# Four graph networks on one core: loops written out, selectors in PSUM, and one count matrix read by transposing DMAs

## What is computed

```python
x = _layernorm(x + _L0_gnn_ref(x, relation_emb, edge_index, edge_type))   # hyperbolic messages, 2 hops
x = _layernorm(x + _L1_gnn_ref(x, edge_index, edge_weight, ...))          # GRU, 2 rounds
x = _layernorm(x + _L2_gnn_ref(x, edge_index, ...))                       # SAGE convolution, 2 layers
x = _layernorm(x + _L3_gnn_ref(x, edge_index, ...))                       # SAGE convolution, 2 layers
```

```python
# L1, round t, with row = src and col = dst
agg = segment_sum(concat([x[col], x[row], edge_attr]) @ msg_W[t].T + msg_b[t], row)
x = gru_cell(agg, x, ...)
# L2, L3, each layer
agg = segment_sum(h[src], dst) * inv_deg
```

## Time and profile before

| | us |
|---|---|
| median of three runs | 22,558.81 |
| the profiled execution | 22,546.55 |
| its span, first to last instruction | 22,544.4 |
| sort, 116 to 3,241 | 3,125 |
| building the matrix, 3,357 to 6,996 | 3,639 |
| hyperbolic passes, each | 3,680 and 3,710 |
| dense pass 2 | 966 |
| dense pass 3, with the transposed copy | 1,999 |

### The profile page before, as it was taken

One profiled execution on the slowest core, in us unless ns is written; L12 is line 12 of the kernel. 1 busy time (PEld: TensorE's weight loads), 2 busy tenths in 40 slices (PEclk: granted clock), 3 DMA queues, 4 the chain that ended last, 5 costly groups with the idle time before them and its releaser, 6 DMA issues. The chain is left out here.

```text
span 22544.4 us, 302048 instructions
## 1 busy us (share of the span) xinstructions
PE 12710.9 (56%) x103818; PEld 11283.5 (50%) x103819; DVE 8510.4 (38%) x15488; ACT 2879.7 (13%) x5263; POOL 8346.1 (37%) x6810
## 2 busy tenths in 40 slices
PE   2222225333322555555555555488777788878887
PEld 1111114333322444444444444388677687878787
DVE  4444446444442555555455555501434400010101
ACT  0000000000001222222122222100343300000000
POOL 4444447888886555554455555300000000000000
PEclk6555556555555555555555555599999999999998
DMA  9600014333332222222222222297899697989798
GB/s 358 272 1 1 1 32 111 77 77 77 77 71 45 71 69 72 71 71 62 69 70 70 70 71 71 54 339 271 297 334 340 236 336 273 316 294 347 263 322 305
DMA packets 2131032, 3586.46 MB, mean 159 GB/s; under 512 B 554444, under 2 KB 1429728, under 8 KB 2037429
## 3 DMA queue, kind: packets, MB, share of 16 engines
q1 hardware_dynamic: 1732405, 3389.59, 42.5%
q0 software_dynamic: 397504, 181.65, 6.6%
HBM read 2672.91 MB, written 907.26 MB: 159 GB/s over the span
## 5 line engine op out<-in xcount | busy, mean ns | idle before, releaser
L762 POOL DMA_INDIRECT room<-table_hyp,pay x3328 | 3430.5, 1031 | 1116.5 <-issue 984.3
L1026 PE MATMUL pair<-room,side 128*128 x6656 | 1688.3, 435 | 2973.9 <-ACT side L1354 2432.6
L1121 PE MATMUL pair<-room,side 128*128 128x192 bf16 x30694 | 3049.1, 250 | 508.0 <-DMA side<-back 327.1
L749 POOL DMA_INDIRECT adj<-sc x1664 | 2962.8, 1781 | 791.9 <-issue 485.3
L1026 PEld LDWEIGHTS pair<-room,side 128*128 128x128 f32 x6656 | 1480.7, 327 | 3287.6 <-issue 3287.6
L1121 PE MATMUL pair<-room,onehot 128*128 128x192 bf16 x31058 | 3006.1, 247 | 110.4 <-DMA onehot<-back 74.8
L1121 PEld LDWEIGHTS pair<-room,side 128*128 128x128 f16 x30694 | 2664.5, 100 | 593.3 <-issue 453.8
L1121 PEld LDWEIGHTS pair<-room,onehot 128*128 128x128 f16 x31058 | 2629.1, 98 | 193.7 <-issue 138.1
L791 POOL DMA_INDIRECT sc<-table_lin,heavy_idx x6 | 5.7, 950 | 6957.4 <-DMA table_lin<-room 6957.4
L734 POOL DMA_INDIRECT payload<-room x1600 | 1554.9, 972 | 1685.7 <-DVEq L1706 1094.9
L2254 DVE TENSOR_REDUCE acc<-pair 128x384 f32 (+2 forms) x314 | 145.3, 526 | 4300.0 <-PE pair L1121 4296.7
(11 more groups left out here) (437 smaller groups left out, 18105.7 us busy)
## 6 DMA issues: line engine op xcount, KB each, us to landing
onehot<-back SPq DMA_DIRECT2D x308, 1024.0 KB, 7.7
side<-back SPq DMA_DIRECT2D x280, 1024.0 KB, 7.7
onehot<-back SPq DMA_DIRECT2D x264, 896.0 KB, 7.1
side<-back SPq DMA_DIRECT2D x240, 896.0 KB, 7.3
onehot<-head_hots SPq DMA_DIRECT2D x208, 1024.0 KB
adj<-xs SPq DMA_DIRECT2D x99, 1728.0 KB
adj<-xs SPq DMA_DIRECT2D x99, 1600.0 KB
side<-adj SPq DMA_DIRECT2D x148, 1024.0 KB, 8.6
```

The costliest lines, as they stand in the source:

```text
L749: pool.indirect_dma_start(out=adj_flat[q // 2][:, :], out_offset=bass.IndirectOffsetOnAxis(ap=edge_to[i % 2][q][:, t:t + 1], axis=0), in_= ...
L762: pool.indirect_dma_start(out=rows[:, h, t, :], out_offset=None, in_=table_hyp[:, :], in_offset=bass.IndirectOffsetOnAxis(ap=pay[:, h, t, ...
L1026: last = nc.tensor.matmul(ps_head[:, j * TW:j * TW + TW], sel_t[:, q % 2, j * P:j * P + P], flat_tab[:, bass.ds(b * TW, TW)], start=True, ...
L1121: last = nc.tensor.matmul(banks[c // 2][:, D3 * (c % 2):D3 * (c % 2) + D3], block_, x3[:, sources[k], :], start=j + k == 0 and c % 2 == 0, ...
```

## The change

Three things at once.

First, all loops over registers become Python loops, and every wait is on a constant; the tick semaphores go. The same work is issued in the same order. Second, `heavy_on` (two selectors of 128x128) moves from SBUF to PSUM, and DVE copies each group's keys to PSUM before it compares with them. Third, there is one matrix `mat`, with the source nodes as rows. The convolutions read it as they read `back`; the GRU passes load it through `dma_start_transpose`; the transposed copy of pass 3 and all that served it go. The heavy row for the GRU passes is a small array of its own, loaded by a plain DMA behind the last unit of each sweep.

```diff
-        def await_reg(eng, who, s, v):
-            eng.wait_ge(s, v)
-            eng.sem_inc(tick[who], 1)
+        def until(eng, s, v):
+            if v > 0:
+                eng.wait_ge(s, v)
...
-                with pool.Fori(0, ITERS - 1) as i:
+                for i in range(0, ITERS - 1):
...
-        heavy_on = [flat_x[:, 1024 + P * k:1024 + P * k + P] for k in range(2)]
+        heavy_on = [bank[2][:, P * k:P * k + P] for k in range(2)]
+        ps_own_keys = [bank[2][:, 2 * P + G * h:2 * P + G * h + G] for h in range(2)]
...
                 dve.drain().then_inc(key_made, 1)
+                V.tensor_copy(ps_own_keys[h], ekey[h])
                 V.tensor_tensor(srcf[h], srcf[h], pad_, ALU.add)
-                V.tensor_scalar(b_, lo_, P - 1, None, ALU.bitwise_and)
-                stt(a_, dstf[h], float(COLS[n % STREAMS // 2]), tile_colf[:, tiles_], ALU.mult, ALU.add)
+                V.tensor_scalar(a_, lo_, P - 1, None, ALU.bitwise_and)
+                V.tensor_scalar(far_block, far_, 7, None, ALU.arith_shift_right)
+                V.tensor_scalar(b_, far_, P - 1, None, ALU.bitwise_and)
+                dve.drain()
+                stt(edge_row, tile_colf[:, tiles_], float(P), a_, ALU.mult, ALU.add)
+                stt(a_, edge_row, float(NB), far_block, ALU.mult, ALU.add)
...
-                V.tensor_tensor(same[h], keys_on[h].rearrange("p (t e) -> p t e", e=P), over(ekey[h], P), ALU.is_equal)
+                V.tensor_tensor(same[h], keys_on[h].rearrange("p (t e) -> p t e", e=P), over(ps_own_keys[h], P), ALU.is_equal)
...
-            for b in range(ADJ_ROWS):
-                for v in range(2):
-                    sp.dma_start(adj[v][P * b:P * b + P, :], zeros_dram[:, 0:COLS[v] * P]).then_inc(zeroed, 16)
+            for v in range(2):
+                for b in range(COLS[v]):
+                    for u in range(2):
+                        half_ = slice(NB * P // 2 * u, NB * P // 2 * u + NB * P // 2)
+                        sp.dma_start(mat[v][P * b:P * b + P, half_], zeros_dram[:, 0:NB * P // 2]).then_inc(zeroed, 16)
+                sp.dma_start(heavy_near[v], zeros_dram[:, 0:COLS[v] * P]).then_inc(zeroed, 16)
...
-                    sp.dma_start(ring[r][:, 0:kn, 0:w * P], mats[half_ if v is None else v][:, k0:k0 + kn, at]).then_inc(unit_here[r], 16)
+                    if v is None:
+                        sp.dma_start_transpose(ring[r][:, 0:far, 0:w * P], mat[half_][near, P * k0:P * k0 + P * far]).then_inc(unit_here[r], 16)
                     else:
...
+                        sp.dma_start(ring[r][:, 0:kn, 0:w * P], mat[v].rearrange("(k p) c -> p k c", p=P)[:, k0:k0 + kn, near]).then_inc(unit_here[r], 16)
+                    if far < kn:
+                        sp.dma_start(ring[r][:, far, 0:w * P], heavy_near[half_][:, near]).then_inc(unit_here[r], 16)
...
-                            flips = turning and k0 + k < NB
-                            if flips:
-                                for t in (turn_act, turn_dve):
-                                    await_(t, NB * s + k0 + k + 1, i, 2 * NB)
...
-                                    flip = nc.tensor.matmul(o[:, P * (c % 4):P * (c % 4) + P], block_, ident16, start=True, stop=True)
```

More of the change, by code:

```diff
@@ L98, with __init__ @@
 class Shape:
-    def __init__(self, units, stages):
+    def __init__(self, units, sweeps):
         self.units = units
-        self.stages = stages
+        self.sweeps = sweeps
         self.n = len(units)
[L106 to L114, removed]
 def far_sources(half_, k):
@@ L728, in _ @@
             pool.wait_ge(filled, GROUPS * 16)
-            with pool.Fori(0, GITERS) as i:
+            for i in range(0, GITERS):
                 for h in range(2):
-                    await_reg(pool, "pool", staged, 2 * i + (h + 1))
+                    until(pool, staged, 2 * i + (h + 1))
                     for c in range(HC):
@@ L975, in _ @@
                     degrees(k, 0, h, h + k == 0)
-            with pe.Fori(1, NITERS + 1) as i:
+            for i in range(1, NITERS + 1):
                 for h in range(2):
@@ L981, in _ @@
                 q_step(i - 1)
-            with pe.Fori(NITERS + 1, GITERS) as i:
+            for i in range(NITERS + 1, GITERS):
                 for h in range(2):
@@ L1072, in run_pass @@
                 fetch_group(m, 0, 0)
-                with pe.Fori(0, ITERS - 1) as i:
+                for i in range(0, ITERS - 1):
                     fetch_group(m, i, 1)
@@ L1179, in gru @@
                 gates(0, 0, False)
-                with pe.Fori(0, NITERS // 2 - 1) as i:
+                for i in range(0, NITERS // 2 - 1):
                     for h in range(2):
@@ L1223, in conv @@
                 second_layer(0, 0, False)
-                with pe.Fori(0, NITERS // 2 - 2) as i:
+                for i in range(0, NITERS // 2 - 2):
                     for h in range(2):
@@ L1395, in run_pass @@
                     pass
-                with act.Fori(0, ITERS - 1) as i:
+                for i in range(0, ITERS - 1):
                     group(2 * i, 0, steps(2 * i + 1, 1))
@@ L1468, in gru @@
                 turned(1, 1)
-                with act.Fori(0, NITERS // 2 - 1) as i:
+                for i in range(0, NITERS // 2 - 1):
                     for h in range(2):
@@ L1501, in conv @@
                 hidden(1, 1, False)
-                with act.Fori(0, NITERS // 2 - 2) as i:
+                for i in range(0, NITERS // 2 - 2):
                     for h in range(2):
@@ L1795, in make_q @@
             def make_q():
-                with dve.Fori(0, NITERS) as i:
+                for i in range(0, NITERS):
                     keep_q(i, 1)
@@ L1801, in _ @@
             rsum(relblk[:, :, D], rel_sq)
-            with dve.Fori(1, NITERS + 1) as i:
+            for i in range(1, NITERS + 1):
                 for h in range(2):
@@ L1811, in _ @@
             dve.drain().then_inc(table_ready, 1)
-            with dve.Fori(NITERS + 1, GITERS) as i:
+            for i in range(NITERS + 1, GITERS):
                 for h in range(2):
@@ L2405, in gru @@
                 stage_blocks(1, 1, False)
-                with dve.Fori(0, NITERS // 2 - 1) as i:
+                for i in range(0, NITERS // 2 - 1):
                     for h in range(2):
```

361 lines of the change are left out of this document (123 added, 238 removed).

## The result

The changed kernel takes 21,236.87 us (median of 4 runs, 21,235.51 to 21,247.06), the kernel before 22,562.22 us beside it: ratio 0.9414, interval 0.9397 to 0.943. It is faster by 1,325 us, a third of the 3,957 us that the sum promised; the time lies in the range, near rival A (21,740).

The account below looks back on a forecast made before the run. No engine was full overall: DMA bound the dense passes, POOL the matrix building, a stall the sort and hyperbolic passes. 22,546.6 - 1,050 - 2,100 - 400 - 407 = 18,590 us; own range 17,700 to 19,500, with rivals 17,700 to 22,000.

Parts of the forecast that it names:

- rival A: Sort and hyperbolic passes: the stall stays, belonging to POOL's back-to-back issue; 21,740 us; chance 0.22, with B 0.05.
- Part 1 and 2: Straight programs without register waits end the stall: -1,050 us in the sort, -2,100 us in the hyperbolic passes.
- the stall: Sort and hyperbolic passes: PE's semaphore updates don't come through while POOL issues DMAs; 27.07 us in one hyperbolic group.
- Part 3: Matrix building: compare operands in PSUM bring the mean accumulating DMA from 1.781 to 1.542 us, -400 us.
- Part 4 and 5: Dense passes 2 and 3: no transposed copy, -1,033 us; transposing loads at 1,279 us a pass; together -407 us.
- my middle: Rate taken for transposing loads in dense passes 2 and 3, between two profile rows: 268 GB/s, 1,279 us a pass.
- the row of 256-byte pieces: Profile row of the output's store, 215 GB/s, taken as slow bound for transposing loads: 1,592 us a pass.
- Part 6: The rest: zeroing, edge additions, loop ends in dense passes, small GRU and convolution loops; 0, at best -50 us.
- B: Dense passes 2 and 3: transposing loads don't overlap, 2,621 us a pass, total 21,270 us; chance 0.13.
- C: Dense passes 2 and 3: each 256-byte row costs 59.9 ns, 5,004 us a pass, total 26,040 us; chance 0.07.

Follow-up runs that it names:

- The fastest version: The changed kernel with POOL waiting for landings after every eighth gather of the hyperbolic passes and every eighth scatter of the sort: 19,563.76 us (0.8674).

## Why the prediction was wrong

*Part 1 and 2, -1,050 and -2,100: the failed step.* I read the stall as "what several register waits at once do to the other engines while POOL issues DMAs". Written out with constants, the kernel before gains 82 us in the sort and 615 in the hyperbolic passes, and the stall stays. The sentence of rival A was the right one: it belongs to POOL's unbroken issue. That the building stage escapes because its DMAs are spaced by 1.85 us fits this, but no run changed that spacing. Against A I set the 40 fast matmuls 54 us after the slow ones, with POOL issuing in both. I had not looked at what POOL did in between. It began a stream of 40 scatters at 1466.69 and the next at 1553.21, after standing still for 36 us:

```profile
1466.69 0.97 POOL L734 DMA_INDIRECT payload<-room  x1 [23.25 <-DVEq L1706]
1553.21 0.97 POOL L734 DMA_INDIRECT payload<-room  x1 [35.77 <-DVEq L1706]
```

PE was slow 38 us into the first stream and fast 5 us into the second. The rows that I held against A speak for it. The sizes can only be compared with the pauses in place. The fastest version has its two passes at 5,538 us where the kernel before has 7,281, and the sort at 2,557 instead of 3,125. That is 2,311 us of the 3,150 that parts 1 and 2 promised; a group takes 53 us and not 47, and POOL's waits for its landings are 7 of these 53.

*Part 3, -400: mechanism right, size off.* The mean of the accumulating DMA is 1,544 ns, the forecast's 1.54 us, and POOL is busy 394 us less. But the stage lost 245 us: 275, as the run with this part alone undone shows, less the 30 by which DVE's new address instructions and the new layout make the stage longer; I had put these at nothing. I counted DVE's waiting as the room for part 3 and left out POOL's own wait, in each of four streams, for its last DMA to land: 91 us in the earlier trace rows, 244 after. A faster issue reaches that landing sooner.

*Part 4 and 5, -407: one term mis-sized.* A plain pass is 937 us as soon as the program is written out. A transposing pass takes 1,427 us, not 1,279: 240 GB/s, within the bounds (966 and 1,592), about half way between my middle and the row of 256-byte pieces. Two passes make 296 us, all of the miss. Against the written-out kernel, no copy and transposing loads are worth 935 + 1,932 - 1,427 - 1,426 = 14 us: what the copy cost, the transposes take back. The Trainium skill, "DMA: Bandwidth & Descriptors", section "Latency and other measured facts", gives 261 GB/s for a non-contiguous middle dimension; that was nearer than my middle (268). For the contiguous case it gives some 350 to 400 GB/s. The measurement doesn't agree: the ring's tile has the gap only in sweeps of 6 and 7 columns, and with it the loads ran at 239 GB/s, without it at 242.

*Part 6, 0 to -50: wrong.* I took the DMA engines as full (share 1.01), so that loop ends could cost nothing. Written out, a plain pass moves 366 GB/s instead of 354; the six passes lose some 230 us and the short steps some 90.

*The sum by its measured terms:* 22,547 - 1,019 (written out) - 303 (PSUM) + 30 (new addresses and layout) - 14 (no copy, transposes) = 21,241 us, against 21,237 measured. The rivals: A was right in its mechanism. Its 21,740 left out the 1,019 us of the written-out program and had parts 3 to 5 520 us too good (807 for 287), hence some 500 us too high. That the time came near it is in part luck: two errors offset each other. B fell: 364 transposing loads take 1,427 us, not 2,621. C fell: by the working of its 59.9 ns, a 256-byte packet took 1.14 x 16 x 1,427 us / 1,326,000 = 20 ns of an engine, not 60.

## What to carry to other kernels

When one engine issues DMAs back to back for tens of microseconds and the others show idle time with nothing awaited or with a "remote" releaser, put a pause into the issue before rewriting anything else: here three waits a group, two lines of code, gave 1,650 us where rewriting 25 loops gave 1,019. Find the length by trial; 8 DMAs (10 us) was best here, 6 and 11 were both 560 us and more behind. And a gain in the issue of a chain of DMAs counts only until the wait for landing ends last. Before a row is held against a rival, look at what the suspected engine did in between.

## What the runs showed of the hardware that was not expected

- PE's semaphore updates reached DVE and ACT 11 and 21 us late while POOL issued indirect DMAs every 1.24 us; with a pause of about 2 us every 5 us they passed within 0.6 us.
- A drain on POOL behind an indirect DMA took 2.3 us, and one before each gather made the kernel 16% slower than before.
- A transposing load ran at 240 GB/s in pieces of 3 and 4 block rows, with a gap in the destination or without (239 and 242), and at 178 GB/s in pieces of one, where SP issued one every 1.33 us; a plain load of the same bytes ran at 365 GB/s.
